# Rotary embedding's exchanged blocks: ScalarE copies in place of four transfers a pair, in the first half of a decoder layer

## The reference, cut to what matters

```python
def _apply_rope(x, cos, sin):
    d = x.shape[-1]
    x1, x2 = (x[..., :d // 2], x[..., d // 2:])
    return jnp.concatenate([x1 * cos - x2 * sin, x1 * sin + x2 * cos], axis=-1)
...
q = split_heads(_bitlinear(x, w_q))
k = split_heads(_bitlinear(x, w_k))
v = split_heads(_bitlinear(x, w_v))
q = _apply_rope(q, cos, sin)
k = _apply_rope(k, cos, sin)
scores = jnp.einsum('bhqd,bhkd->bhqk', q, k) * scale
...
probs = jax.nn.softmax(scores, axis=-1)
y = jnp.einsum('bhqk,bhkd->bhqd', probs, v)
return _bitlinear(y, w_o)
```

## Time and profile before

| | us |
|---|---|
| median of 3 runs | 2307.34 (2306.18 to 2309.06) |
| profiled execution | 2305.53, its span 2303.4 |
| first half, until all engines have ended it | about 1613 of the span |
| TensorE busy over the span | 2089.3 (91%) |
| VectorE | 1722.5 (75%) |
| ScalarE | 1161.2 (50%) |
| GpSimd | 992.3 (43%) |

### The profile page before, as it was taken

One profiled execution on the slowest core, in us unless ns is written; L12 is line 12 of the kernel. 1 busy time (PEld: TensorE's weight loads), 2 busy tenths in 40 slices (PEclk: granted clock), 3 DMA queues, 4 the chain that ended last, 5 costly groups with the idle time before them and its releaser, 6 DMA issues. The chain is left out here.

```text
span 2303.4 us, 51845 instructions
## 1 busy us (share of the span) xinstructions
PE 2089.3 (91%) x19560; PEld 1356.4 (59%) x19560; DVE 1722.5 (75%) x4655; ACT 1161.2 (50%) x2662; POOL 992.3 (43%) x924
## 2 busy tenths in 40 slices
PE   1565899999999999999999999997889999999989
PEld 1344566666666666666666666665455555555544
DVE  8998777777787777777777777766577777777664
ACT  6786534433333343343333334334666766676661
POOL 4343334333333343344333333423556565655551
PEclk9877899999999999999999999998899999999999
DMA  8877665756556656656566566568978777787752
GB/s 237 180 149 150 127 131 142 151 125 158 138 138 140 144 133 149 143 131 150 132 155 143 129 155 138 123 158 212 218 164 212 170 197 182 182 197 165 163 119 70
DMA packets 738169, 357.09 MB, mean 155 GB/s; under 512 B 684152, under 2 KB 684408, under 8 KB 737920
## 3 DMA queue, kind: packets, MB, share of 16 engines
q1 hardware_dynamic: 737920, 353.77, 66.1%
HBM read 104.11 MB, written 49.28 MB: 67 GB/s over the span
## 5 line engine op out<-in xcount | busy, mean ns | idle before, releaser
L905 POOL TENSOR_TENSOR halves<-prob,halves 128x384 f16<-128x384 f32 x256 | 236.2, 923 | 577.5 <-ACT halves L824 577.5
L68 PE MATMUL ps_j<-xT,wT 128*128 128x256 f16 x3634 | 416.8, 275 | 21.9 <-DMA wT<-rows_qkv 21.9
L68 PEld LDWEIGHTS ps_j<-xT,wT 128*128 128x128 f16 x3634 | 359.1, 99 | 82.7 <-issue 22.2
L98 DVE CUSTOM_DVE_ANT_0 prob<-ps_s,mask 128x128 f32<-128x128 f32 (+1 forms) x1024 | 304.8, 354 | 135.7 <-PE ps_s L88 132.0
L104 ACT ACTIVATE prob<-prob,negmax 128x128 f32<-128x128 f32 x512 | 202.0, 394 | 260.3 <-DVE negmax L98 259.3
L1064 DVE TENSOR_TENSOR raw<-raw,cos 128x512 f32<-128x512 f32 x128 | 137.0, 1071 | 246.7 <-DMA swp<-raw 246.7
L813 ACT ACTIVATE raw<-ps_j,factor_qk 128x256 f32<-128x256 f32 x158 | 66.2, 470 | 447.8 <-PE ps_j L68 447.8
L68 PE MATMUL ps_t<-xT,wT 128*128 128x256 f16 x2254 | 255.8, 274 | 0.0
L105 ACT ACTIVATE prob<-prob,negmax 128x256 f32<-128x256 f32 x512 | 252.9, 494 | 0.0
L1593 POOL TENSOR_TENSOR halves<-prob,halves 128x768 f16<-128x768 f32 x128 | 210.6, 1645 | 91.8 <-ACT halves L1537 91.6
L68 PEld LDWEIGHTS ps_t<-xT,wT 128*128 128x128 f16 x2254 | 221.4, 98 | 36.6
(11 more groups left out here) (211 smaller groups left out, 3815.3 us busy)
## 6 DMA issues: line engine op xcount, KB each, us to landing
swp<-raw SPq DMA_DIRECT2D x512, 64.0 KB, 2.0
xin<-in_x SPq DMA_DIRECT2D x33, 512.0 KB, 4.5
x_kept<-after_self_attention SPq DMA_DIRECT2D x16, 1024.0 KB, 5.6
xres<-in_x SPq DMA_DIRECT2D x31, 512.0 KB, 4.3
after_self_attention<-xres SPq DMA_DIRECT2D x30, 512.0 KB, 3.3
queries<-q2T SPq DMA_DIRECT2D x30, 512.0 KB, 3.1
out<-x SPq DMA_DIRECT2D x10, 1024.0 KB, 4.6
kv_ahead<-in_ctx SPq DMA_DIRECT2D x9, 1024.0 KB, 5.7
```

Of the source, the lines that this page charges most:

```text
L68: last = pe.matmul(out, lhs(t[0], a), rhs(t[1], a), start=a == 0 and t is terms[0], stop=a == n_tiles - 1 and t == (0, 0))
L98: dve.tensor_tensor_reduce(scores[:, cols], bank[:, cols], hidden, scale, NO_SCORE, ALU.add, ALU.min, least[:, n:n + 1]).then_inc(done, 1)
L905: pool.tensor_tensor(halves[:, e, 1, :], prob[:, e], halves[:, e, 0, :], ALU.subtract).then_inc(prob_lo, 1)
```

## The change

SP's `swap` goes away. ScalarE does the exchange itself, right behind the projection of the same pair: it waits for its own writes of `raw` and for rot_done of the rotation before, and then copies four blocks of 32 partitions by 512 numbers to their partners' partitions. VectorE's `rotated` waits for these four copies by one semaphore.

```diff
-            def swap(g):
-                p = g % 2
-                sp.wait_ge(raw_done, g + 1)
-                if g > 0:
-                    sp.wait_ge(rot_done, g)
-                for a in range(4):
-                    sp.dma_start(swp[32 * a:32 * a + 32],
-                                 raw[32 * (a ^ 1):32 * (a ^ 1) + 32, p]) \
-                        .then_inc(swapped[p], 16)
...
-                if g < GP:
-                    swap(g)
...
                 last.then_inc(raw_done, 1)
+
+                act.wait_ge(raw_done, g + 1)
+                if g > 0:
+                    act.wait_ge(rot_done, g)
+                for a in range(4):
+                    act.activation(swp[32 * a:32 * a + 32], raw[32 * (a ^ 1):32 * (a ^ 1) + 32, g % 2],
+                                   ACT.Copy).then_inc(swapped, 1)
...
-                dve.wait_ge(swapped[g % 2], 64 * (g // 2 + 1))
+                dve.wait_ge(swapped, 4 * g + 4)
```

More of the change, by code:

```diff
@@ L388, in self_attention @@
         q_out = sem("q_out")
-        swapped = [sem(f"swapped{p}") for p in range(2)]
+        swapped = sem("swapped")
         j_ready = sem("j_ready")
```

## The result

The changed kernel takes 2344.03 us (median of 4 runs, 2340.97 to 2350.68), the kernel before beside it 2306.76 us (4 runs, 2301.29 to 2309.06). The ratio is 1.0162, 95% interval [1.0143, 1.0181]: slower by 37 us. The forecast was 2314 with a range up to 2321, so the sign was right and the time, 23 us above the top of the range, was not. The profiled execution took 2340.97 us, its span is 2338.8 us, 35.4 more than before.

What follows compares the result with a forecast made beforehand. VectorE was taken to bound the first 300 us, TensorE the stretch from 300 to 1500. Start +8.2, steady stretch +0.5 and end -1.5 sum to +7.2 us, 2314.5, put down as 2314; range 2303 to 2321.

Steps and rivals of the forecast that it cites:

- What bounds the kernel: VectorE sets the pace from 60 to 300 us; TensorE, busy 1199.57 of 1200 us, from 300 to 1500.
- The set of copies: On ScalarE: four copies of 0.62 us, neighbours overlapping by 0.10, take 2.2 us a set; bounds 0.6 to 4.5.
- The steady stretch: 300 to 1500 us: rotation begins 1.5 us earlier for no gain, exponentials move later; +0.5 us, between -1 and +3.
- Rival C: Steady stretch: earlier rotation meets GpSimd's two subtractions of probabilities; +15 us, about 2329; chance 0.10.
- The exponentials' price: Steady stretch: exponentials 1.8 us later (2.3 behind a value tile); late transposes hold TensorE 0.1 to 0.5 us each.
- The start: First 300 us: copies ahead of weight rows wait for late rotations; lateness cumulates to +8.2 us, between 3 and 12.
- place 2: Start, VectorE's compares at 181.95 and 203.92 us wait for weight rows behind copies: +2.95, then +5.1 us cumulated.
- place 1: Start, first value tile's copy behind two sets of copies ends at 84.9; VectorE wanted it at 83.04: +1.85 us.
- 3, value subtraction: Start: copies, rows and value tile follow a late rotation; VectorE's value subtraction moves from 222.45 to 229.9: +7.45 us cumulated.
- 4, last tile: Start: the last weight tile's load goes out late; VectorE starts the tile at 262.0 instead of 253.77: +8.2 us cumulated.
- rival A: ScalarE absorbs the copies into its waits from 60 to 300 us; about 2303 us; chance 0.20.
- The end: Last pair of the first half: about 3 us of VectorE's transfer wait returns, half taken: -1.5 us, between -3 and +2.

Runs made afterwards that it cites:

- e5: Changed kernel with one ScalarE copy of all 128 partitions, blocks not exchanged, in place of the four copies; ratio to the kernel before 0.9997.
- e3: Changed kernel with ScalarE's value tile ahead of the four copies from pair 13 on; ratio to the kernel before 1.0067.
- e4: Changed kernel with GpSimd's subtraction of x cut to 64 of 1024 columns from the seventh tile on; ratio to the kernel before 1.0072.
- e10: Kernel before, with ScalarE copies behind the value tile from pair 13 on, transfers in pairs 0 to 12; ratio to the kernel before 1.0015.
- e11: Kernel before, with copies only in pairs 0 to 12, behind first rows and value tile, ahead of the exponentials; ratio to the kernel before 1.0007.
- e7: Changed kernel with copies as the step's last work in steps 0 to 12, behind the value tile from 13; ratio to the kernel before 1.0084.
- e8: Kernel before, with copies last in steps 0 to 12 and behind the projection in the last two pairs, transfers between; ratio to the kernel before 1.0055.
- e6: Changed kernel with each of the four 32-partition copies onto its own partitions, nothing exchanged; 2351.94 us in one run.

## Why the prediction was wrong, step by step

**What bounds the kernel** was read right: VectorE sets the pace of the start, TensorE of the rest, and VectorE's 226.6 us wait for transfers cost nothing.

**The set of copies**: 0.62 us each was right (0.627), the overlap of 0.10 was not. The set takes 2.58, not 2.2. The Trainium skill, ScalarE: Activation LUTs, What ACT_TABLE_LOAD costs, gives 186 ns plus 0.833 ns per element for an activation with immediate scale and bias, by which I estimate 0.61 us for 512. The trace agrees (0.627 and 0.632). The Trainium skill says in the same section that neighbours overlap by about 93 ns. The trace agrees for the 128-partition copy of e5 (0.64 long, the next instruction starts 0.53 us behind its start) and disagrees for four copies of 32 partitions (4 x 0.627 = 2.51, measured 2.58). By that overlap I estimate 2.2 for the set.

**The steady stretch is the step that failed.** It said: the rotation can begin 1.5 us earlier, the gain is nothing, and the price falls on the exponentials. The first clause was worked out on a pair with no value tile, at 603 us. There it nearly held: the rotation begins 3.48 us after the projection in place of 4.7. In the steps with a value tile, every second one, it begins 5.33 us after the projection, and in the 28 pairs that lose it began after 5.05 in the median before. So 1.5 us were forecast as gained and 0.3 were lost. VectorE's value subtraction stands before the rotation in its order and needs ScalarE's value tile, which I had counted as queued behind the copies only when I moved the exponentials (the 2.3 in place of 1.8 us). The same queue was seen at two places of the start and not carried over to the stretch in which it occurs every second pair. e3 shows that with the value tile ahead 25.7 of the 30.3 us go.

**Rival C** named the partner rightly, GpSimd, and was sized with that same gain: at worst 1.8 us longer against 1.5 us earlier, so 0.3 us against a slack of 0.6. Longer the rotation became, by 1.15 us in the 28 pairs (5.52 to 6.67), less than the 1.8; the 1.5 us earlier didn't come. It ends at 12.00 us after the projection in place of 10.71, 1.3 us later against a slack of 0.4. The subtraction of x, which C doesn't name, lay beside the rotation before too; with that subtraction cut to 64 columns the rotation is 4.86 us long (e4) and the loss is gone. The Trainium skill, Perfetto Trace Analysis, Optimizing Scalar/DVE Operations, says that GpSimd and VectorE share a read port; the trace agrees, the cast takes 0.43 us without the subtraction of x beside it and 2.23 with it (e4 against the changed kernel). The rule had been quoted behind the rival and given a tenth of the chance.

**The exponentials' price** was mis-sized: +0.5 us, bounded by +3, against +4.6 (e3) and +5.3 (e10), where nothing else is left in the stretch. The set is 0.4 us longer than assumed, and a transpose that is late costs 0.7 us in the mean (5.6 in 8 waits), not 0.1 to 0.5.

**The start** was right in its mechanism, and from place 2 on close; place 1 was a third of what was forecast:

| place | predicted | measured |
|---|---|---|
| 1, first value tile | +1.85 | +0.63 (83.67) |
| 2, compare | +2.95 | +3.43 (185.38) |
| 2, compare at 203.92 | +5.1 | +5.29 (209.21) |
| 3, value subtraction | +7.45 | +8.25 (230.70) |
| 4, last tile | +8.2 | +7.57 (261.34) |

I ended the reckoning there, with "from there TensorE is full". It wasn't: behind the last tile's reduction its scales took 1.72 us beside GpSimd's subtraction of x (0.23 at this place before), and the value subtraction at 278.72 waited another 4.09 us for rows and copies. At pair 11 it is +10.8, inside the bound of 12. That coupling and not load is the cause is shown by e11, where the copies stay and the loss goes; and rival A (ScalarE absorbs them) would have been right for that other place in the order. e7 and e8 show the opposite error: put too late in the step, the same copies hold back the rotation in place of the rows.

**The end** was right: -3.3 us at pair 127, -1.9 when the second half begins (41.1 to 39.1), against -1.5 with "half of that" given back. That it agrees so well is partly luck: the half was a guess.

**Sum**: +8.2 + 0.5 - 1.5 was forecast, +10.8 + 30.3 - 1.9 came, and -3.7 of the second half that nothing here explains. Of the 28 us between the sum forecast and the span measured, the steady stretch alone accounts for 29.8, the start for 2.6; the end and the second half take 4.1 back.

## What to carry to other kernels

When work is put ahead of others on an engine, list everything queued behind it and who waits for each, in every kind of step of the loop, not in the one step whose timeline was read; the neighbour here was half of all steps. Two pieces of work that used to be released by different engines at different times can end up released by the same instruction, and then they run beside each other: look for pairs of engines that slow each other. A slowed instruction costs nothing while its chain still ends in time (e5), so add up start and length against the engine that waits. And before a change is given up, try its other places in the order: the same 512 copies cost 37 us behind the projection and 6 us behind the value tile.

## What was not expected of the hardware

Four ScalarE copies of 32 partitions by 512 numbers don't overlap: 0.625 to 0.632 us each (512 of them), 2.58 a set, while a 128-partition copy of the same width lets the next instruction begin 0.11 us before its end. Whether they cross partitions makes no difference (e6, one run). Whether the cause is the small number of partitions or the change of partitions from one to the next wasn't tried.

```profile
L809 ACT ACTIVATE swp<-raw x512: 625/628/632, 59.4 to 1614.6; 32x512 f32<-32x512 f32 x171
```

The slowing between VectorE and GpSimd goes both ways and differs from instruction to instruction: beside GpSimd the sine multiply takes 1.40 in place of 0.68 us, the cast 2.23 in place of 0.43, and a tiny 128x8 product 1.72 in place of 0.23, while GpSimd's 128x384 subtraction goes from 0.92 to 1.26 us in the mean.
